# A convolution stage whose result is added to x by VectorE from PSUM, with the sums over head elements shared out anew

## The reference

```python
def _L0_xattn_ref(k, v, q, ssm_kernel, D, head_dim):        # head_dim 8, so 32 heads
    kv = jnp.einsum('bhil,bhjl->bijhl', k_, v_)             # k = v = context
    ...                                                     # causal convolution along l, per head
    out = y + kv * D[None, None, None, :, None]
    out = jnp.einsum('bijhl,bhil->bjhl', out, q_)           # q = layernorm(x)
...
x = x + jnp.tanh(g_xattn[0]) * _L0_xattn_ref(ctx_2048, ctx_2048, _layernorm(x), ...)
x = x + jnp.tanh(g_ffn[0]) * _L0_ffn_ref(_layernorm(x), ...)   # 8-bit rows, ternary weights
x = x + jnp.tanh(g_xattn[1]) * _L1_xattn_ref(_layernorm(x), ctx_2048, mask)
x = x + jnp.tanh(g_ffn[1]) * _L1_ffn_ref(_layernorm(x), ...)
```

## Time and profile before

| what | value |
|---|---|
| median of 3 runs | 693.62 us (692.9 to 693.78) |
| the profiled execution, own time | 695.11 us |
| its span, first to last instruction | 693.3 us |
| mean granted clock of TensorE | 0.997 of full speed |
| busy: PE, DVE, ACT, POOL | 678.9, 582.7, 414.9, 295.0 us |
| VectorE starts step 2, step 3, step 12, step 15 | 33.06, 46.65, 136.40, 169.45 us |
| TensorE starts the second stage | 173.00 us |

### The profile page before, as it was taken

The page is one execution under the profiler, slowest core; times in us unless marked ns, Lnnn a source line. Parts: engine busy times, 40 slices in busy tenths (PEclk is TensorE's granted clock), DMA queues, the critical chain, the costliest instruction groups (busy, mean ns, idle before and its releaser), DMA issues.

```text
span 693.3 us, 12921 instructions
## 1 busy us (share of the span) xinstructions
PE 678.9 (98%) x4826; PEld 357.8 (52%) x4826; DVE 582.7 (84%) x1054; ACT 414.9 (60%) x646; POOL 295.0 (43%) x455
## 2 busy tenths in 40 slices
PE   9989999999999999999999999999999999999997
PEld 6756555555444444567754444444444444444445
DVE  5979999998998998658958889988888888898891
ACT  3689999856679989748667444434434434434440
POOL 6869999999765544537400521111110111110000
PEclk9999999999999999999999999999999999999999
DMA  8797775553379789998042243363332334342234
GB/s 296 222 293 209 227 188 141 148 148 111 102 167 194 187 167 201 218 357 308 17 136 17 61 94 75 91 92 92 76 90 41 68 92 92 77 78 59 61 71 112
DMA packets 155390, 94.85 MB, mean 137 GB/s; under 512 B 133825, under 2 KB 134337, under 8 KB 155329
## 3 DMA queue, kind: packets, MB, share of 16 engines
q1 hardware_dynamic: 153600, 90.02, 51.8%
q0 software_dynamic: 1200, 3.93, 1.7%
q10 hardware_dynamic: 528, 0.09, 0.1%
HBM read 53.04 MB, written 8.47 MB: 89 GB/s over the span
## 4 chain that ended last, share of the span: by engine, by line
PE 68%; POOL 15%; DVE 6%; issue 3%; ACT 2%; DMA 1%; SPq 0%; POOLq 0%; ACTq 0%
PE psum L955 29%; PE psum L987 15%; PE psum L882 9%; POOL phase_space L583 5%; PE psum L894 4%; PE psum L938 4%; PE psum L916 4%; POOL phase_space L600 3%; POOL x_sb L607 2%; POOL phase_space L586 2%; POOL phase_space L603 1%; PE psum L740 1%; PE psum L971 1%; DMA x_sb<-x_between 1%; POOL ln_rs L302 1%
## 5 line engine op out<-in xcount | busy, mean ns | idle before, releaser
L955 PE MATMUL psum<-phase_space 128*128 128x512 f16 x1024 | 223.8, 379 | 0.1
L955 PEld LDWEIGHTS psum<-phase_space 128*128 128x128 f16 x1024 | 100.0, 98 | 122.2 <-issue 1.7
L740 PE MATMUL psum<-phase_space 64*64 64x288 f32 x2304 | 150.3, 409 | 6.3 <-POOL phase_space L586 3.5
L740 PEld LDWEIGHTS psum<-phase_space 64*64 64x64 f32 x2304 | 89.9, 134 | 61.0 <-POOL phase_space L586 8.5
L712 POOL DMA_DIRECT2D out<-x_sb x15 | 9.3, 621 | 234.6 <-DVE x_sb L1516 234.6
L987 PE MATMUL psum<-phase_space 128*128 128x512 f16 x480 | 105.7, 379 | 0.0
L1281 ACT ACTIVATE phase_space<-psum,b_scalars 128x512 f32<-128x512 f32 x64 | 43.4, 682 | 75.2 <-PE psum L955 75.1
L1287 ACT ACTIVATE phase_space<-phase_space,magic 128x1024 f32<-128x1024 f32 x32 | 36.4, 1148 | 77.3 <-DVE phase_space L1500 77.3
L882 PE MATMUL psum<-phase_space 128*128 128x512 bf16 (+1 forms) x384 | 78.8, 361 | 0.7 <-DVE phase_space L1343 0.7
L987 PEld LDWEIGHTS psum<-phase_space 128*128 128x128 f16 x480 | 47.0, 98 | 56.6
L1485 DVE SCALAR_TENSOR_TENSOR phase_space<-psum,b_scalars,phase_space 128x512 f32<-128x512 f32 x64 | 47.7, 748 | 28.4 <-ACT phase_space L1281 28.3
(11 more groups left out here) (123 smaller groups left out, 1081.7 us busy)
## 6 DMA issues: line engine op xcount, KB each, us to landing
phase_space<-in_L_weights SPq DMA_DIRECT2D x24, 512.0 KB, 6.0
phase_space<-in_L_weights SPq DMA_DIRECT2D x12, 704.0 KB, 7.1
phase_space<-kpad SPq DMA_DIRECT2D x14, 512.0 KB, 4.3
phase_space<-in_context_heads SPq DMA_DIRECT2D x15, 384.0 KB, 5.2
x_sb<-in_x_tiles SPq DMA_DIRECT2D x16, 256.0 KB, 4.8
phase_space<-in_context_turned SPq DMA_DIRECT2D x8, 512.0 KB, 5.9
x_between<-x_sb SPq DMA_DIRECT2D x16, 256.0 KB
x_sb<-x_between SPq DMA_DIRECT2D x16, 256.0 KB, 6.8
```

The lines of the kernel that those rows point to most:

```text
L740: return nc.tensor.matmul(at(dst, 0, [[64, B], [1, NP]]), toep[n % 2][row:row + Q, hh, shift:shift + Q], kv[n % 2][row:row + Q, IN_SLOT[j] ...
L955: last = nc.tensor.matmul(bank(2 * (m % 3) + w), fb_qT[n % 2][:, kk % 2, kk // 2, :], b_wT[w][:, kk // 2, c * 512:(c + 1) * 512], start=(k ...
```

## The change

The 40 values of a head are summed elsewhere. For head 0 GpSimd does everything (`reduce_first_head`: the fold of 512 elements, then its two additions). For head 1 VectorE does everything in one `tensor_reduce` (`reduce_second_head`): 256 sums of 5 values each that lie 8 words apart in `prod`. `s_res` becomes one semaphore per head.

In steps 2 to 15 VectorE adds tanh of the gate times bank 4 to x in one instruction, put after the second of the four product instructions of head 0. ScalarE's `copy_result` and GpSimd's `add_result` are gone from the loop; they stay for the last two results. Part (1, 0) of `conv_head` now waits for that addition (`s_r0`).

On SyncE the transposing DMA of steps 1 to 13 moves ahead of the weight loads.

```diff
@@ -452,6 +452,8 @@
                         load_x(n + 4)
                     if n + 2 < NT:
                         load_context(n + 2)
+                    if 1 <= n < NT - 2:
+                        turn_q_planes(n + 2)
                     for w, first in ((0, 0), (1, 2)):
                         if n in (first, first + 1):
                             load_weight(w, 2 * (n - first))
@@ -461,8 +463,8 @@
                     if n == 0:
                         sp.wait_ge(s_dadd, 1)
                         sp.dma_start(kpad[:, :], kp_sb).then_inc(s_kpad, 16)
+                        turn_q_planes(2)
                     if n + 2 < NT:
-                        turn_q_planes(n + 2)
                         load_toeplitz(n + 2)
                     if n in B_EARLY:
                         load_b(B_EARLY[n])
@@ -591,19 +593,23 @@
                     nc.gpsimd.tensor_scalar(ln_off[:, n:n + 1], ln_ag[:, 0, n, 0:1], ln_rs[:, 0, n:n + 1], -1.0,
                                             ALU.mult, ALU.mult).then_inc(s_off, 1)
 
-                def finish_heads(n, hh):
-                    pool.wait_ge(s_fold2, 2 * n + hh + 1)
+                def reduce_first_head(n):
+                    pool.wait_ge(s_prod, 2 * n + 1)
+                    pr = prod[n % 2][0]
+                    rows = LB * B
+                    nc.gpsimd.tensor_tensor(at(pr, 0, [[SLOTS, rows], [1, 16]]), at(pr, 0, [[SLOTS, rows], [1, 16]]),
+                                            at(pr, 16, [[SLOTS, rows], [1, 16]]), ALU.add).then_inc(s_fold2, 1)
                     if n >= 3:
                         pool.wait_ge(s_rt, n - 2)
-                    pr = prod[n % 2][hh]
-                    dst = at(res[n % 3].rearrange("p l c -> p (l c)"), hh * E, [[2 * E, LB * B], [1, E]])
-                    nc.gpsimd.tensor_tensor(dst, at(pr, 0, [[SLOTS, LB * B], [1, E]]), at(pr, E, [[SLOTS, LB * B], [1, E]]),
+                    dst = at(res[n % 3].rearrange("p l c -> p (l c)"), 0, [[2 * E, rows], [1, E]])
+                    pool.wait_ge(s_fold2, n + 1)
+                    nc.gpsimd.tensor_tensor(dst, at(pr, 0, [[SLOTS, rows], [1, E]]), at(pr, E, [[SLOTS, rows], [1, E]]),
                                             ALU.add).then_inc(s_fold3, 1)
-                    pool.wait_ge(s_fold3, 2 * n + hh + 1)
-                    nc.gpsimd.tensor_tensor(dst, dst, at(pr, 32, [[SLOTS, LB * B], [1, E]]), ALU.add).then_inc(s_res, 1)
+                    pool.wait_ge(s_fold3, n + 1)
+                    nc.gpsimd.tensor_tensor(dst, dst, at(pr, 32, [[SLOTS, rows], [1, E]]), ALU.add).then_inc(s_res[0], 1)
 
                 def add_result(n):
-                    pool.wait_ge(s_re, n + 1)
+                    pool.wait_ge(s_re, n + 3 - NT)
                     nc.gpsimd.tensor_tensor(x_sb[:, n, :], x_sb[:, n, :], rt[n % 2], ALU.add).then_inc(s_r0, 1)
 
                 def a_norm(t):
@@ -659,15 +665,12 @@
                     if n >= NT - 2:
                         a_integers_x(n + 2 - NT)
                     if n >= 1:
-                        finish_heads(n - 1, 1)
+                        reduce_first_head(n - 1)
                     if n >= NT - 3:
                         a_norm(n + 3 - NT)
                     if n + 3 < NT:
                         ln_root(pool, 0, n + 3)
                         conv_offset(n + 3)
-                    if n >= 2:
-                        add_result(n - 2)
-                    finish_heads(n, 0)
 
                 for t in range(NT + 1):
                     if t == 1:
@@ -725,7 +728,8 @@
                     last.then_inc(s_xt, 1)
 
                 def turn_result(n, to, freed):
-                    pe.wait_ge(s_res, 2 * n + 2)
+                    pe.wait_ge(s_res[0], n + 1)
+                    pe.wait_ge(s_res[1], n + 1)
                     pe.wait_ge(s_prod, freed)
                     for lb in range(LB):
                         cols = at(bank(to), lb * P, [[1, P]]) if lb % 2 == 0 else at(bank(to), lb * P + Q, [[-Q, 2], [1, Q]])
@@ -775,7 +779,7 @@
                     if n == 0 and hh == 1:
                         pe.wait_ge(s_qc, 2)
                     if n >= 2 and hh == 1:
-                        pe.wait_ge(s_re, n - 1)
+                        pe.wait_ge(s_r0, n - 1)
                     conv_part(n, hh, 1, 0)
                     pe.wait_ge(s_rows, left + 2)
                     conv_part(n, hh, 7, 2)
...
@@ -1109,8 +1113,6 @@
 
                 def copy_result(n, bk):
                     act.wait_ge(s_rt, n + 1)
-                    if n >= 2:
-                        act.wait_ge(s_r0, n - 1)
                     nc.scalar.activation(rt[n % 2], bank(bk), ACT.Copy, scale=gates[:, 0:1]).then_inc(s_re, 1)
 
                 def sum_weight(w, j):
@@ -1226,8 +1228,6 @@
                         nc.scalar.activation(gates[:, :], gates[:, :], ACT.Tanh).then_inc(s_tanh, 1)
                         act.wait_ge(s_tanh, 1)
                         act.wait_ge(s_const, 6)
-                    if n >= 2:
-                        copy_result(n - 2, 4)
                     for w in range(3):
                         for j in range(4):
                             if ABS_STEP[w, j] == n:
@@ -1326,7 +1326,7 @@
                     dve.wait_ge(s_y, 2 * n + hh + 1)
                     dve.wait_ge(s_qc, n + 1)
                     if n >= 2:
-                        dve.wait_ge(s_res, 2 * n - 3 + hh)
+                        dve.wait_ge(s_res[hh], n - 1)
                     y = psum[:, 4 * hh:4 * hh + 4, :].rearrange("p l c -> p (l c)")
                     q = q_ext[n % 3][:, hh, :]
                     pr = prod[n % 2][hh]
@@ -1335,6 +1335,12 @@
                                             at(q, 0, [[EX, rows], [1, 4], [1, E]]), ALU.mult)
                     nc.vector.tensor_tensor(at(y, NP, [[64, rows], [E, 3], [1, E]]), at(y, E, [[64, rows], [E, 3], [1, E]]),
                                             at(q, 0, [[EX, rows], [0, 3], [1, E]]), ALU.mult)
+                    if n >= 2 and hh == 0:
+                        dve.wait_ge(s_rt, n - 1)
+                        if n == 2:
+                            dve.wait_ge(s_tanh, 1)
+                        nc.vector.scalar_tensor_tensor(x_sb[:, n - 2, :], bank(4), gates[:, 0:1], x_sb[:, n - 2, :],
+                                                       ALU.mult, ALU.add).then_inc(s_r0, 1)
                     nc.vector.tensor_tensor(at(pr, 32, [[SLOTS, rows], [4, 2], [1, 4]]),
                                             at(y, 32, [[64, rows], [0, 2], [1, 4]]),
                                             at(q, 4, [[EX, rows], [4, 2], [1, 4]]), ALU.mult).then_inc(s_fold, 1)
@@ -1342,12 +1348,13 @@
                     side = at(pr, 1, [[SLOTS, rows], [9, 3], [1, E]])
                     nc.vector.tensor_tensor(side, side, at(y, NP, [[64, rows], [E, 3], [1, E]]), ALU.add).then_inc(s_prod, 1)
 
-                def fold_heads(n, hh):
-                    dve.wait_ge(s_prod, 2 * n + hh + 1)
-                    pr = prod[n % 2][hh]
-                    rows = LB * B
-                    nc.vector.tensor_tensor(at(pr, 0, [[SLOTS, rows], [1, 16]]), at(pr, 0, [[SLOTS, rows], [1, 16]]),
-                                            at(pr, 16, [[SLOTS, rows], [1, 16]]), ALU.add).then_inc(s_fold2, 1)
+                def reduce_second_head(n):
+                    dve.wait_ge(s_prod, 2 * n + 2)
+                    if n >= 3:
+                        dve.wait_ge(s_rt, n - 2)
+                    nc.vector.tensor_reduce(at(res[n % 3].rearrange("p l c -> p (l c)"), E, [[2 * E, LB * B], [1, E]]),
+                                            at(prod[n % 2][1], 0, [[SLOTS, LB * B], [1, E], [E, 5]]), AX.X, ALU.add
+                                            ).then_inc(s_res[1], 1)
 
                 def a_weight_mean(w):
                     dve.wait_ge(s_tot, w + 1)
@@ -1374,9 +1381,9 @@
...
@@ -1564,7 +1571,6 @@
                     if n in TOT_STEP:
                         a_weight_mean(TOT_STEP[n])
                     products(n, 0)
-                    fold_heads(n, 0)
                     if n in TOT_STEP:
                         w = TOT_STEP[n]
                         dve.wait_ge(s_mean, 2 * w + 1)
@@ -1585,7 +1591,7 @@
                         dve.wait_ge(s_wa, 4 * w + 4)
                         nc.vector.tensor_reduce(tot[:, w:w + 1], a_abs[:, w, :], AX.X, ALU.add).then_inc(s_red, 1)
                     if n < NT - 1:
-                        fold_heads(n, 1)
+                        reduce_second_head(n)
 
                 for t in range(NT):
                     a_product(t, 0)
@@ -1595,7 +1601,7 @@
                     if 1 <= t < NT - 3:
                         a_stats(t + 3)
                     if t == 0:
-                        fold_heads(NT - 1, 1)
+                        reduce_second_head(NT - 1)
                         a_scale_x(2)
                     a_product(t, 2)
                     if t == 0:
```

10 lines of the change are left out of this document (5 added, 5 removed).

## The result

The changed kernel takes 711.55 us, median of 4 runs (710.91 to 712.17), against 693.43 us for the kernel before (4 runs): a ratio of 1.0261, 95% interval 1.0244 to 1.0277. It is 18 us slower; forecast were 689.2 us, and the range ended at 705.

The account below looks back on a forecast made before the run. GpSimd was taken to set the 10.20 us step, VectorE just behind. Terms -0.4, -3.2, -2.4, +0.15 and +1.4 gave -4.45 us, applied to the 693.62 us median: 689.2 us, range 686.8 to 705.

Parts of the forecast that it names:

- the price of the reduction: VectorE's head 1 reduction of 1280 elements, taken at 1.05 ns each plus 135 ns fixed: 1.48 us.
- The high bound: VectorE's reduction with each element counted twice: 2.82 us.
- the rival at 2.15 us: The hop costs: reduction midway between the bounds, 0.67 us more in 14 steps and tail, 699 to 702 us; chance 0.42.
- Start to step 2, -0.4: Before step 2: two folds and a wait become one 1.39 us reduction, about 0.2 us less in each of two steps.
- Step 2, -3.2: Third step: ScalarE's late copy is out of the way, 10.4 us instead of 13.59.
- Steps 3 to 11, -2.4: Middle steps: VectorE sets nine steps of 9.63 us plus 0.7 for weight sums, 87.4 us instead of 89.75.
- hardly any idle: Sign of being right: VectorE's steps 3 to 11 about 9.63 us apart with almost no idle time.
- Steps 12 to 14, +0.15: Late steps: TensorE stands about 1.5 us for the addition, VectorE some 0.6 for head 1; 33.2 us against 33.05.
- the tail, +1.4: Step 15 to next stage's tile 2: VectorE's last products 0.6 us later, reduction 0.8 us more than a fold.
- The clock rival: End of stage: TensorE's new stands in steps 13 to 15 lower its clock; two falls, 3.2 us, 692.4 us; chance 0.07.
- The early gain doesn't come: Step 2: weights or Toeplitz matrix late instead, gain 0 to 1 us, time 691.5 to 692.5 us; chance 0.05.

Follow-up runs that it names:

- adjacent: The changed kernel with VectorE's second-head reduction reading five adjacent words per sum instead of words eight apart (sums wrong, time only): 694.29 us, 1.0016 of before.
- second profile: The kernel before, unedited, profiled once more: 693.54 us in this execution.

## Why the prediction was wrong

**The step that failed is the price of the reduction.** "I take 1.48" had 2.52 us in its place. The high bound was 2.82 and the rival at 2.15 us had 0.42, so the mechanism was on the table with its sign. I chose the low end by products that read in runs of 8 and 4 adjacent words, and they do not bear on it: a run of four says nothing on a run of one. The only source that priced one, the cited section of the Trainium skill, came to 2.3 us by my estimate. The range ended at 705 because I cut the rival at 2.4 us. Putting 2.52 into the rival's own rule, 1.04 us on each of 15 places, gives 693.6 - 4.45 + 15.6, some 705, and with its 3 us for standing longer 708. The table says where the 21.5 us between "forecast" and "after" lie: 18.7 between "adjacent" and "after", which is 1.04 us for each reduction from step 3 to step 14 (9.31 + 3.12), 2.26 for the two at the start, 2.61 at the end of the stage with the fallen clock in it (1.64 us on thirty records), and 1.4 in the rest; the other 2.75 are the terms below.

**The other terms, against the table.**
- *Start to step 2, -0.4.* The adjacent version has 32.64, which is the forecast to 0.02 us; the change pays two hops.
- *Step 2, -3.2.* 10.94 us instead of 10.4; the wait for ScalarE's copy is gone as forecast. But 2.1 us of the gain belonged to the one execution that was profiled: in the second profile the step takes 11.50 (of which the steps 3 to 11 give back 0.66). I carried the gain over to the median by subtraction; that counts a stand and a fallen clock which the second profile, close to the median, doesn't have. Without this the sum gives 690.7, not 689.2.
- *Steps 3 to 11, -2.4.* VectorE sets the step, as forecast: 9.63 us by the sum, 9.88 with the reduction at 1.49. Most of what is missing is the 0.2 us between the statistics and head 1, which goes when the addition stands first; I had it as no cost in the middle steps ("hardly any idle"). With the reduction at 2.52 us the stretch takes 98.21. GpSimd was freer than forecast, busy for some 7.3 us a step (60.56 of 90 us) where I had 8.6.
- *Steps 12 to 14, +0.15, and the tail, +1.4.* Without the hop 33.62 and 16.64 instead of 33.2 and 15.85; both waits were forecast (1.5 us for TensorE, measured 1.34 but only 0.44 in step 13; 0.6 us for VectorE, measured 0.96). A stand of TensorE of 1.06 us for a DMA ahead of tile 2 was not. What I missed is that the two waits form a loop that a reordering would break. With the hop they grow to 36.74 and 19.25.
- *The clock rival* came, once, after the stand of 2.38 us before 183.57, and cost the 1.6 us that it had; without the hop it did not come.
- *The early gain doesn't come:* half true, and not by late DMAs: most executions of the kernel before do not have the loss that was to be won back.

Open: 1.0 us more from tile 2 to the end than before. TensorE waits there for DMAs for 1.9 us in all, against 0.7 in the second profile of before and in the adjacent version; why those DMAs land later no run shows.

## What to carry to other kernels

Price an access pattern by a row with the same run length (how many adjacent words are read before the next hop), and where none exists, let the range hold the whole price to its upper bound: here one pattern of strides decided the sign. Look at what an instruction reads besides how much: with two inputs in SBUF a fold took half as long again or twice as long beside a busy GpSimd (medians 0.97 and 1.46 us against 0.66), the reduction with one input did not. And take a profile of before a second time before crediting a change with the removal of a stall that one execution shows.
